# Second attention: split probabilities in 8 of 18 units a head, outputs rounded out of PSUM, weight pieces in units 6 to 13, maxima a unit later

## The reference

```python
q = ln @ Wq.T                                            # ln: layernormed x, 1024 rows a batch
kv = concatenate([xn @ Wkv.T, ln @ Wlkv.T], axis=1)      # 77 context rows and 1024 rows
k, v = kv[..., :INNER], kv[..., INNER:]
qn = rmsnorm(q, qn_g) * SCALE
kn = rmsnorm(k, kn_g)
attn = einsum('bhid,bhjd->bhij', qn, kn)                 # 1024 x 1101 for each b and h
attn = softmax(where(full_mask, attn, -max), axis=-1)
out = einsum('bhij,bhjd->bhid', attn, v)
x = x + out.transpose(0, 2, 1, 3).reshape(b, m, INNER) @ Wo.T + bo
```

## Time and profile before

| | |
|---|---|
| median of three runs | 929.47 us (927.81 to 930.09) |
| the profiled execution | 928.22 us |
| its span, first to last instruction | 926.5 us |
| TensorE busy in the span | 866.8 us, 94% |
| VectorE, ScalarE, GpSimd busy | 630.7, 532.6, 388.9 us |
| mean granted TensorE clock | 0.987 |

### The profile page before, as it was taken

How to read it: one execution, slowest core, us unless ns; L and a number is a source line. 1 busy time by engine, 2 the same in 40 slices (tenths; PEclk the granted TensorE clock), 3 DMA queues, 4 the chain that set the end, 5 groups by cost and what they waited for, 6 DMA issues and landing times.

```text
span 926.5 us, 14997 instructions
## 1 busy us (share of the span) xinstructions
PE 866.8 (94%) x4299; PEld 611.3 (66%) x4300; DVE 630.7 (68%) x1275; ACT 532.6 (57%) x851; POOL 388.9 (42%) x334
## 2 busy tenths in 40 slices
PE   9977789889999999999999999999999999999992
PEld 4635455545555555555457887878888888888881
DVE  5788987855567557456488779846666666666666
ACT  2558885445665765775554534326666666666650
POOL 2144455435676746756515545512222222222210
PEclk9999999989999999999999999999999999999997
DMA  9400000009478578569565100078711298526405
GB/s 310 110 1 1 0 1 1 1 5 364 160 292 328 194 305 326 219 269 350 199 262 196 82 1 1 12 316 342 305 40 36 71 348 341 208 88 254 116 9 182
DMA packets 49909, 154.07 MB, mean 166 GB/s; under 512 B 6266, under 2 KB 24438, under 8 KB 44236
## 3 DMA queue, kind: packets, MB, share of 16 engines
q1 hardware_dynamic: 46124, 144.25, 41.4%
q0 software_dynamic: 3744, 9.31, 3.1%
HBM read 97.85 MB, written 56.62 MB: 167 GB/s over the span
## 4 chain that ended last, share of the span: by engine, by line
PE 67%; DVE 17%; ACT 6%; issue 3%; DMA 3%; POOL 2%; SPq 1%; DVEq 0%; ACTq 0%; POOLq 0%
PE banks L1047 11%; PE banks L1300 8%; PE banks L1302 8%; PE banks L1301 8%; PE banks L1015 4%; PE banks L1039 3%; PE banks L1040 3%; DVE small L2105 2%; PE banks L1337 2%; PE banks L1339 2%; PE banks L1338 2%; PE banks L1313 2%; PE banks L953 2%; PE banks L919 1%; PE banks L1061 1%
## 5 line engine op out<-in xcount | busy, mean ns | idle before, releaser
L1047 PE MATMUL banks<-wexp 128*65 128x512 f32 (+1 forms) x288 | 149.9, 602 | 3.5 <-ACT wexp L1614 3.5
L677 POOL TENSOR_TENSOR cv_hl<-wexp,cv_hl 128x1024 fp32r<-128x1024 f32 x45 | 108.6, 2421 | 56.0 <-ACT cv_hl L1591 55.4
L1300 PE MATMUL banks<-ring,x_hi 128*128 x312 | 127.5, 408 | 0.0
L1302 PE MATMUL banks<-ring,x_lo 128*128 x312 | 122.1, 391 | 0.0
L1301 PE MATMUL banks<-ring,x_hi 128*128 x312 | 122.0, 391 | 0.0
L1614 ACT ACTIVATE wexp<-banks 128x512 f32<-128x512 f32 x128 | 76.4, 599 | 64.2 <-PE banks L1040 63.8
L2105 DVE TENSOR_REDUCE small<-banks 128x1 bf16<-128x1107 f32 x64 | 84.1, 1314 | 38.4 <-PE banks L1015 38.4
L1750 ACT ACTIVATE banks<-wexp 128x1024 f32 x72 | 73.5, 1021 | 47.7 <-DVE aux L2496 47.7
L1728 ACT ACTIVATE aux<-banks 128x512 f32<-128x512 f32 x78 | 46.7, 599 | 61.2 <-PE banks L1302 45.2
L1039 PE MATMUL banks<-q_hi,k_hl 128*128 128x512 f32 x144 | 76.7, 533 | 1.9 <-ACT q_lo L1582 1.0
L1302 PEld LDWEIGHTS banks<-ring,x_lo 128*128 128x128 f32 x312 | 58.6, 188 | 13.2
(11 more groups left out here) (374 smaller groups left out, 2171.5 us busy)
## 6 DMA issues: line engine op xcount, KB each, us to landing
wsplit<-cv_hl SPq DMA_DIRECT2D x45, 1024.0 KB, 8.0
ring<-wsplit SPq DMA_DIRECT2D x32, 1280.0 KB
wexp<-in_L_ffn_w SPq DMA_DIRECT2D x40, 512.0 KB, 5.9
wexp<-in_expert_biases SPq DMA_DIRECT2D x8, 1152.0 KB, 6.6
ring<-wsplit SPq DMA_DIRECT2D x4, 1024.0 KB, 8.2
wexp<-moe_y SPq DMA_DIRECT2D x7, 512.0 KB, 6.1
wexp<-in_L_ffn_sw SPq DMA_DIRECT2D x5, 512.0 KB, 9.0
x_sb<-in_x SPq DMA_DIRECT2D x4, 512.0 KB, 7.6
```

The costliest lines, as they stand in the source:

```text
L677: g.tensor_tensor(sides(hl[:, PIECE:2 * PIECE]), raw, sides(hl[:, 0:PIECE]).bitcast(f32), ALU.subtract).then_inc(s['cv_lo'], 1)
L1047: mm(pb[5 + half][0:DA, :], vh[b][0:w, c, :], pT[q % 3][0:w, :], start=c == 0, stop=c == len(KTILES) - 1).then_inc(s['a_pv'], 1)
L1300: mm(o[:], x_hi[u][:, kc, :], hi, start=kc == 0 and not primed, stop=False, skip_group_check=primed)
L1302: last = mm(o[:], x_lo[u][:, kc, :], hi, start=False, stop=primed and kc == KC - 1, skip_group_check=primed)
```

## The change

The units of key tiles 0, 1, 2 and 7 (`SPLIT_UNITS`: 0 to 5, 14, 15; in the last step only 0 to 5) get split probabilities. ScalarE writes exp twice, once rounded into `p_hi` and once in full over the scores in PSUM; VectorE subtracts (`chances_low`) to `p_lo`. `values` becomes three float32r matmuls: `v_hi` by `p_hi`, `v_lo` by `p_hi`, and one unit later (`values_low`) `v_hi` by `p_lo`. The other units stay as they are. A head's outputs are rounded by ScalarE straight from PSUM (`outputs_hi` in every step), their remainder is taken by VectorE (`outputs_low`), GpSimd makes two 32-row copies (`outputs_dup`), and the rows of `wo_1` and `wo_2` are laid out for it. The weight pieces move to units 6, 7, 8, 9, 11 and 13, the maxima to units 6 to 13, the joined outputs to units 7 to 14. The core of the diff:

```diff
-        CONV_AT = (3, 5, 7, 9, 11, 13)
+        SPLIT_UNITS = tuple(2 * c + half for c in SPLIT_TILES for half in range(2))
+        SPLIT_LAST = SPLIT_UNITS[:6]
+        PER_HEAD = 2 * (TB + 1) + len(SPLIT_UNITS)
+        CONV_AT = (6, 7, 8, 9, 11, 13)
...
 # GpSimd
-            g.memset(wo_1[0:DH, :, D:D + 2].bitcast(f32), 0.0)
-            link(g.memset(wo_1[DH:P, :, :].bitcast(f32), 0.0))
-            for row in (DH, DH + 32):
-                link(g.memset(wo_1[row:row + 1, :, D:D + 1].bitcast(f32), 1.0))
+            for w in (wo_1, wo_2):
+                link(g.memset(w[:, :, D:D + 2].bitcast(f32), 0.0))
+                link(g.memset(w[DH:DUP, :, 0:D].bitcast(f32), 0.0))
+                link(g.memset(w[DH:DA, :, D:D + 1].bitcast(f32), 1.0))
...
             def head_values(h, b):
+                for at, src in tiles:
+                    last = g.tensor_copy(v_hi[b][:, at, 0:DH], src)
+                link(last)
+                for at, src in tiles:
+                    g.tensor_tensor(v_lo[b][:, at, 0:DH], src, v_hi[b][:, at, 0:DH].bitcast(f32), ALU.subtract)
...
+            def outputs_dup(n):
+                pool.wait_ge(s['a_ohi'], 2 * n + 2)
+                link(g.tensor_copy(o_hi[DUP:P, :], o_hi[0:DH // 2, :].bitcast(f32)))
+                g.tensor_copy(o_x[DUP:P, :], o_hi[DH // 2:DH, :].bitcast(f32)).then_inc(s['a_odup'], 1)
...
 # TensorE
-            def scores(n, b, q):
+            def scores(n, b, q, last):
-                if q >= 2 or not isinstance(n, int) or n > 0:
-                    pe.wait_ge(s['a_p'], n * NU + (q - 1))
+                if q >= 2 and q - 2 in split_units(last):
+                    pe.wait_ge(s['a_plo'], n * len(SPLIT_UNITS) + SPLIT_UNITS.index(q - 2) + 1)
+                elif q >= 2:
+                    pe.wait_ge(s['a_p'], n * PER_HEAD + exps_done(q - 2, last))
...
+                if q in split_units(last):
+                    o, k = pb[5 + half][0:DA, :], SPLIT_TILES.index(c)
+                    mm(o, v_hi[b][:, k, :], p_hi[q % 3], start=c == 0, stop=False)
+                    mm(o, v_lo[b][:, k, :], p_hi[q % 3], start=False, stop=False).then_inc(s['a_pv'], 1)
+                    return
...
+            def values_low(n, b, q, last):
+                c, half = divmod(q, 2)
+                pe.wait_ge(s['a_plo'], n * len(SPLIT_UNITS) + SPLIT_UNITS.index(q) + 1)
+                mm(pb[5 + half][0:DA, :], v_hi[b][:, SPLIT_TILES.index(c), :], p_lo[q % 3], start=False, stop=False).then_inc(s['a_pv'], 1)
...
-                lag, head_at = (3 if first else 0), 5
+                lag, head_at = (3, 5) if first else (0, 6)
-                    if q == 0 and not first:
-                        pe.wait_ge(s['a_o'], n)
+                    if q < 2 and not first:
+                        pe.wait_ge(s['a_olo'], 2 * n - 1 + q)
-                    values(n, b, q)
+                    values(n, b, q, last)
+                    if q - 1 in split_units(last):
+                        values_low(n, b, q - 1, last)
-                    if 6 <= q < 5 + TB and not first and not last:
-                        joined(n - 1, h_last, out_at, q - 6)
+                    if 7 <= q < 7 + TB and not first and not last:
+                        joined(n - 1, h_last, out_at, q - 7)
...
 # ScalarE, step
-                    if q < 2 * TB:
+                    if q in split_units(last):
+                        a(p_hi[q % 3], pb[3 + q % 2][:], ACT.Exp).then_inc(s['a_p'], 1)
+                        a(pb[3 + q % 2][:], pb[3 + q % 2][:], ACT.Exp).then_inc(s['a_p'], 1)
+                    elif q < 2 * TB:
                         a(pT[q % 3], pb[3 + q % 2][:], ACT.Exp).then_inc(s['a_p'], 1)
-                    if q == 0 and not first:
-                        act.wait_ge(s['a_o'], n)
-                        a(o_hi[0:DA, :], oT[0:DA, :], ACT.Copy).then_inc(s['a_ohi'], 1)
-                    if q == NU - 1 and last:
-                        outputs_hi(0, n)
+                    if q == NU - 1:
+                        outputs_hi(0, n, last)
-                    outputs_hi(1, n)
+                outputs_hi(1, n, last)
-                    a(oT[0:DA, 0:512], pb[5][0:DA, :], ACT.Copy)
-                    a(oT[0:DA, 512:S], pb[6][0:DA, :], ACT.Copy).then_inc(s['a_o'], 1)
...
 # VectorE
+            def outputs_low(n, half):
+                ve.wait_ge(s['a_ohi'], 2 * n + half + 1)
+                at = slice(half * 512, (half + 1) * 512)
+                v.tensor_tensor(o_x[0:DA, at], pb[5 + half][0:DA, :], o_hi[0:DA, at].bitcast(f32), ALU.subtract).then_inc(s['a_olo'], 1)
+
+            def chances_low(n, q, last):
+                ve.wait_ge(s['a_p'], n * PER_HEAD + exps_done(q, last))
+                v.tensor_tensor(p_lo[q % 3], pb[3 + q % 2][:], p_hi[q % 3].bitcast(f32), ALU.subtract).then_inc(s['a_plo'], 1)
...
+                if not first:
+                    for half in range(2):
+                        outputs_low(n - 1, half)
+                ahead = 4 if first else 1
+                for q in range(6):
+                    chances_low(n, q, last)
+                    if q >= ahead and not last:
+                        low(n + 1, 1 - b, q - ahead)
                 if not last:
-                    for k in range(5):
+                    for k in range(6 - ahead, 5):
                         low(n + 1, 1 - b, k)
                 for t in range(TB + 1):
                     if not last and t < TB:
                         maximum(n + 1, t)
                     if not first and t > 0:
                         joined(use if last else use + 5, 1 - b, t - 1, last)
+                    if t == TB - (2 if first else 1) and not last:
+                        chances_low(n, 14, last)
+                if not last:
+                    chances_low(n, 15, last)
                 if more:
                     scaled(h_next, b)
```

More of the change, by code:

```diff
@@ L220, in program @@
         vh = [scr.take((TB + 1) * DA, TB + 1) for _ in range(2)]
+        scr.at = even(scr.at)
+        assert scr.at == PT_AT
         pT = [scr.take(512) for _ in range(3)]
@@ L225, in program @@
         scr.take(S)
+        assert scr.at == VS_AT
+        scr.take(2 * B * NT * DA)
         assert scr.at <= RING * WSP - SPLIT
@@ L240, in program @@
         assert RING * WSP + ax.at == WO2_AT
-        ax.take(NH * D)
+        wo_late = ax.take(NH * (D + 2), NH)
         mask_no = ax.take(SKB)
@@ L409, in hidden_done, with split_units, exps_done, values_done @@
                 eng.wait_ge(s['h_fP'], ci + 1)
-        CONV_AT = (3, 5, 7, 9, 11, 13)
+        SPLIT_UNITS = tuple(2 * c + half for c in SPLIT_TILES for half in range(2))
+        SPLIT_LAST = SPLIT_UNITS[:6]
+        PER_HEAD = 2 * (TB + 1) + len(SPLIT_UNITS)
+        def split_units(last):
+            return SPLIT_LAST if last else SPLIT_UNITS
+        def exps_done(q, last, full=True):
+            return q + 1 + sum(k < q for k in split_units(last)) + (full and q in split_units(last))
+        def values_done(q, last, low):
+            split = split_units(last)
+            return q + 1 + sum(k < q - 1 for k in split) + (low and q in split) * (1 + (q - 1 in split) + 1)
+        CONV_AT = (6, 7, 8, 9, 11, 13)
         CONV_END = (3, 5, 7)
@@ L443, in _ @@
             load(wcT[0:DCR, 1, :], W['L1_xattn_Wkv'][P:DC, :], 'ld_l1')
-            for r in (0, DH):
-                load(wo_raw[r:r + DH], W['L1_xattn_Wo'].rearrange("(h d) n -> d h n", d=DH), 'ld_l1')
+            wo_rows = W['L1_xattn_Wo'].rearrange("(h d) n -> d h n", d=DH)
+            load(wo_raw[0:DH], wo_rows, 'ld_l1')
+            load(wo_raw[DUP:P], wo_rows[0:DH // 2], 'ld_l1')
+            load(wo_late[DUP:P, :, 0:D], wo_rows[DH // 2:DH], 'ld_l1')
             load(bo1_all[:], W['L1_xattn_bo'].partition_broadcast(P), 'ld_l1')
@@ L1084, in step @@
                 minus_at = use + 5 if first else use + 5 + TB
-                lag, head_at = (3 if first else 0), 5
-                scores(n, b, 0)
+                lag, head_at = (3, 5) if first else (0, 6)
+                scores(n, b, 0, last)
                 for q in range(NU):
                     if q + 1 < NU:
-                        scores(n, b, q + 1)
+                        scores(n, b, q + 1, last)
                     if q == lag and not last:
@@ L1092, in step @@
                             turned(n + 1, use, 1 - b, k)
-                    if q == 0 and not first:
-                        pe.wait_ge(s['a_o'], n)
+                    if q < 2 and not first:
+                        pe.wait_ge(s['a_olo'], 2 * n - 1 + q)
                     if 6 <= q < 6 + TB // 2 and last:
                         joined(n - 1, h_last, out_at, 2 * (q - 6))
-                    if q == 6 + TB and not first and not last:
-                        joined(n - 1, h_last, out_at, TB - 1)
-                    values(n, b, q)
+                    values(n, b, q, last)
+                    if q - 1 in split_units(last):
+                        values_low(n, b, q - 1, last)
```

(4 more changed lines are left out.)

121 lines of the change are left out of this document (72 added, 49 removed).

## The result

The changed kernel took 970.9 us, median of four runs (970.2 to 975.2), against 929.1 in the four runs beside it (927.8 to 930.1): 1.046 times the time, 95% interval 1.044 to 1.049. The direction is the forecast's. The size is not: +42 where +15 was forecast, and outside its range. The profiled execution took 970.22 us (before 928.22), its span 968.5, the mean granted clock 0.968 (before 0.987).

A forecast was written before the change was run, and what follows sets the result against it. TensorE was taken as the bound, by 0.15 us a unit in the maxima loop. Seven heads at 2.2 and -0.5 for the last gave +14.9 on 928.22; with 1.25 for the median, 944 us, range 928 to 957.

The forecast's parts named there:

- 7 x 2.2 = 15.4: Seven heads with weight pieces: TensorE idles about unit 10 behind the late fourth piece, 2.2 us a head.
- rival 3: Clock: each head's stop of 2.5 us drops TensorE to the 1.2 GHz level, giving 962 us; chance 0.08.
- the slot wait: ScalarE's piece p + 3 waits for piece p's store; slot cycle 10.2 us, 6.6 after GpSimd; chance 0.68.
- +2.2 forecast: Step 0, first head of the second attention: the same 2.2 us as each of seven heads with pieces.
- The tail's working: Head's end: scores 16 and 17 wait for VectorE's subtractions of units 14 and 15; next head at 7.0 us.
- Start to first reduction, "+0.4": From a head's start to its first maxima reduction: 11.9 us where it was 11.5, so +0.4 a head.
- TensorE alone: 11.5 - 6 x 0.17 + 1.33 = 11.8: Check of the head's start: six splits save 0.17 us each, one more unit costs 1.33.
- The tail, "-0.45": From last reduction to the next head: 7.0 us where it was 7.45, so -0.45 a head.
- It is idle until unit 6, so nothing: GpSimd in each head: its four added small instructions cost nothing.
- the preparation of `wo`, "nothing": GpSimd's longer preparation, about 4.3 us, lies inside 15.9 us of idle and costs nothing.
- The last head: Last head: splits, its pieces in units 3 and 5 and fewer end subtractions: -0.5 us, between -1.7 and +1.
- The first two rivals: First: TensorE stays the bound, slots don't matter, 918 us, chance 0.14; second: break-even, about 931, chance 0.10.

The follow-up runs named there:

- third experiment: The kernel before with only the weight pieces moved, from units 3, 5, 7, 9, 11, 13 to 6, 7, 8, 9, 11, 13: 950.3 us.
- ninth experiment: The changed kernel with SyncE issuing a piece's store ahead of the load three pieces on: 972.9 us.
- the sixth: Experiment 5's kernel with step 0's `scaled(0, 1)` in three parts behind the subtractions of units 1, 2 and 3: 941.4 us.
- the first experiment: The changed kernel with the weight pieces moved two units apart, to units 6, 8, 10, 12, 14, 16: 951.9 us.
- 5: The first experiment's kernel with step 0's VectorE subtractions of units 14 and 15 taken one reduction earlier: 943.7 us.
- 4: The changed kernel with GpSimd's last two `wo` preparation instructions held back until VectorE has scaled the last group: 971.3 us.
- 13: The kernel before with two unused casts and a subtraction, 4.4 us, added on GpSimd behind its `wo` preparation: 930.5 us, ratio 1.0022.
- 15: The sixth's kernel, pieces in 6, 8, 10, 12, 13, 15, splits only in 0 to 3, maxima copied first, last `wo` work in step 0: 932.1 us.
- the eighth experiment: The changed kernel with the weight pieces in units 6, 8, 9, 11, 13, 14: 949.6 us.
- 2: The changed kernel with the weight pieces back in units 3, 5, 7, 9, 11, 13 and GpSimd's key copy after two pieces again: 950.8 us.
- 7: The changed kernel with eight unused matmuls ahead of the values of unit 10 in each head with pieces: 969.1 us.
- 16: The changed kernel with raw weight loads cut from 512 to 64 KB from the fourth piece on, so not the real weights: 954.6 us.

## Why the forecast was wrong

**The clock and heads with pieces, "7 x 2.2 = 15.4": mechanism right, two things mis-sized.** ScalarE's fourth piece does wait about 4 us, TensorE does stop 2.2 us near unit 10, and moving the pieces alone is enough for stops of 1.5 to 2.0 (third experiment). In steps 1 to 6 the maxima stretch grew by 18.7 us where 13.2 was forecast. In steps 4 to 6, at full clock, it was 2.1 to 2.6 a head, my number. In steps 1 to 3 it was 3.7, 4.5 and 3.3: the low clock behind the stop, rival 3. I had argued that TensorE "is full up to the stop"; it is, and the clock fell in three heads all the same, and stayed in three others with stops of 1.8 to 2.4 us. What decides between the two is open, and the length of the stop alone doesn't: the stops were 2.25, 3.06 and 2.18 us where it fell, 1.83, 2.25 and 2.36 where it didn't. In the ninth experiment it fell behind 2.31, 2.36 and 2.39 and not behind 2.45, 2.84 and 2.36, and in the sixth it fell once behind waits of 0.75 and 0.36 (TensorE, the end of step 4 and the start of step 5; eight transposes take 1.89 where they take 1.04 elsewhere):

```profile
379.34 1.07 PE L1111 MATMUL banks<-wexp 77*65 77x512 f32 x2 [0.75 <-ACT wexp L1694]
380.78 0.71 PE L1098 MATMUL banks<-q_hi,k_hl 128*128 128x512 f32 x1 [0.36 <-ACT q_lo L1655]
...
382.57 1.89 PE L1057 MATMUL banks<-ident,wexp 128*128 128x128 f32 x8
```

The section "HAM oscillation" of "TensorE: Matmul & The Clock Gate" (Trainium skill) has a loop that waits some 3 to 5 us for a DMA in each turn and falls to the low clock in each turn. The stops here are shorter, and the trace agrees with it in half of the turns.

**What stands behind the slot wait.** I took 6.6 us from the earlier trace rows as a property of one slot. It is what DMA needs when pieces follow one another: 1.5 MB each at about 400 GB/s. That the number held is in part luck: the earlier trace rows was itself read where pieces followed one another. The section "The DMA setup-cost knee" of "SBUF — State Buffer" (Trainium skill) counts each transfer alone: 2 us and its bytes. By that the store of 1 MB alone would take 4.4, an estimate. With the loads cut to 64 KB it took 4.6 us to land, near that; in the full bunch it took 8.2, and there the trace does not agree. Inside one head both show: in step 4 of the changed kernel the first store, with nothing but its own piece's load ahead of it, lands in 5.9 us and the third in 9.4. Pieces two units apart don't end this either (7.4 us, median of the first experiment's stores); what ends is the wait, as a slot is wanted later.

**Step 0 was counted as one of seven equal heads, and this failed most: +2.2 forecast, +15.9 measured.** I had put all eight heads at about 34.0; step 0 took 39.2 in the kernel before already. In the code, step 0 has its maxima two units later (`lag` 3), and the root and `scaled(0, 1)` stand ahead of its first subtraction on VectorE. The tail's working ("scores 16 wait for the first, scores 17 for the second") was done for a head whose last reduction is over when the subtraction of 14 is due. In step 0 it isn't. Experiments 1, 5 and 6 give 4.2 + 9.4 + 2.5.

**Start to first reduction, "+0.4" taken, +1.15 measured a head.** The units came as worked out: in the first experiment's step 3 the scores of units 2 to 5 are 1.6 apart, those of unit 7 start 10.2 after the head's, where my units add up to 10.15. What failed is the last term. From the scores of the unit behind the first maxima to the first reduction it is 342.48 to 344.85 in step 3 of the changed kernel, 2.4 us; my 11.9 left 1.75 for it. A part of the difference is a matmul that I had no place for: the late third of unit 5, 0.23, stands in unit 6 ahead of the first maxima (TensorE, kernel before, then changed kernel):

```profile
347.83 0.80 PE L1039 MATMUL banks<-q_hi,k_hl 128*128 128x512 f32 x1
348.47 0.39 PE L1040 MATMUL banks<-q_lo,k_hi 65*128 65x512 f32 x1
```

```profile
342.48 0.50 PE L1098 MATMUL banks<-q_hi,k_hl 128*128 128x512 f32 x1
342.82 0.40 PE L1099 MATMUL banks<-q_lo,k_hi 65*128 65x512 f32 x1
343.05 1.02 PE L1111 MATMUL banks<-wexp 128*65 128x512 f32 x2
343.51 0.79 PE L1117 MATMUL banks<-p_lo,v_hi 128*65 128x512 f32 x1
```

The row at 347.83 is stretched, 0.80 for 0.40, so the second matmul of the scores is the better mark: from it to the first reduction it is 1.80 before (348.47 to 350.27) and 2.03 after (342.82 to 344.85). By the same mark my check, "TensorE alone: 11.5 - 6 x 0.17 + 1.33 = 11.8", fails too: of the 6 x 0.17 = 1.02 some 0.6 has come by the scores of unit 6 (9.65 after the head's start before, 9.04 after), as those of unit 2 come no sooner (3.0 in both), and unit 5 takes 1.54 where I had 1.3.

**The tail, "-0.45" a head: right**, -2.7 us in six heads.

**"It is idle until unit 6, so nothing" and the preparation of `wo`, "nothing": the second failed.** The work is hidden for GpSimd and not for VectorE, which stands while GpSimd subtracts. Only the added memsets had been given bounds, 0 to 1.1; the profile shows +3.35 at the first scores of step 0. Experiments 4 and 13 show the contention, 13 and 15 put its price at 1.4 and 2.2 us of the median. The 3.35 itself is one execution's. In the eighth experiment, whose instructions up to step 0 are those of the changed kernel, the scalings take 2.81 and TensorE waits for them just as long, and yet step 0 starts at 195.37, where it started before (195.43):

```profile
39.80 2.81 DVE L1951 TENSOR_SCALAR aux<-x_sb,small 128x256 f32<-128x256 f32 x4
...
42.67 1.09 PE L906 MATMUL banks<-ident,aux 128*128 128x128 f32 x8 [1.64 <-DVE aux L1951]
...
195.37 0.47 PE L1098 MATMUL banks<-q_hi,k_hl 128*128 128x512 f32 x1 [0.72 <-issue]
```

In the ninth, with the same instructions up to there again, it starts at 202.66. What differs is the mean granted clock from 40 to 90 us: 0.97 in the kernel before and in the eighth, 0.86 in the changed kernel, 0.80 in the ninth. So up to 7.3 us between two executions go with where the clock falls there, and a difference of 1 to 3 us between two medians is to be read with that in mind.

**The last head: within its bounds** (-0.2, forecast -0.5).

**The first two rivals** fall: TensorE did not stay the bound, and nothing came near break-even.

## What to carry to other kernels

Before counting a loop's cost times its turns, read the first turn's order by itself: peeled turns have other lags, and what is harmless in the loop can stand in the way there. Price a buffer wait by the bytes of the burst behind it (here 1.57 MB a piece at about 400 GB/s) and not only by the slot's own round trip: spreading the same pieces over the head won 19 us. Idle time of GpSimd is not free for work that reads and writes SBUF while VectorE does the same on the critical path.

## What the runs showed of the hardware

- While GpSimd ran a subtraction with both operands in SBUF, these instructions of VectorE in SBUF stood until it ended: a 77 x 2 one took 2.15 us for 0.17 and four scalings 2.82 to 3.01 for 1.38 (beside 2.18 to 2.34 us of GpSimd), two multiplications 4.55 for 2.35 (beside a piece's 2.42, which took 3.26). Subtractions out of PSUM beside a piece stayed at 0.68 to 0.69.
- Stops of about 2 us made TensorE's clock fall to its 1.2 GHz level in some heads and not in others of the same loop (granted 0.83 to 0.87 over the 10 us from the stop in steps 1 to 3, 1.00 in 4 to 6). Waits of 0.75 and 0.36 us were followed by the low level too, once in six heads of the sixth experiment. A pair of stops of 2.13 and 2.00 us, 5 us apart, cost 9.4 us.
- With the same instructions ahead of it, step 0 started at 195.4 to 202.7 us in eight profiled executions (the changed kernel and experiments 1, 2, 5, 7, 8, 9 and 16); the mean granted clock from 40 to 90 us was 0.97 in the earliest and 0.80 in the two latest.
- SyncE's nine small loads of `bias_b` in step 3 took 5.2 us to issue and held up the store of a piece behind them.
